# Who multiplies the last tile's branches by their mixture weights: VectorE in two wide calls, or ScalarE in sixteen narrow ones

## What is computed

```python
# _gate: four weights per token and head
w = jax.nn.softmax(logits / t, -1)
w = jnp.maximum(w, floor)
w = w / w.sum(-1, keepdims=True)
# behind it, in _L0_attn_ref: the sum of the branches by their weights,
# a root-mean-square norm over the 64 channels of each head, then the projection Wo
```

## Time and profile before

| what | value |
|---|---|
| median of 3 runs | 1334.34 us (1330.45 to 1338.84) |
| profiled execution, its own time | 1321.46 us |
| its span, first to last instruction | 1319.8 us |
| PE busy | 1152.2 us, 87% of the span |
| DVE busy | 806.1 us, 61% |
| ACT busy | 547.3 us, 41% |
| POOL busy | 395.3 us, 30% |

### The profile page before, as it was taken

The page is one execution under the profiler, slowest core; times in us unless marked ns, Lnnn a source line. Parts: engine busy times, 40 slices in busy tenths (PEclk is TensorE's granted clock), DMA queues, the critical chain, the costliest instruction groups (busy, mean ns, idle before and its releaser), DMA issues.

```text
span 1319.8 us, 25278 instructions
## 1 busy us (share of the span) xinstructions
PE 1152.2 (87%) x10204; PEld 826.6 (63%) x10204; DVE 806.1 (61%) x1542; ACT 547.3 (41%) x965; POOL 395.3 (30%) x637
## 2 busy tenths in 40 slices
PE   3778599899988998889997999889997999887828
PEld 3644485488636884378745885478735885477427
DVE  6753266765766565765776666765775666653253
ACT  1154236443563335443463336533463336531312
POOL 6007300941058100751038200841048100840000
PEclk9988799989998998989998999989997999985758
DMA  5040104010131103010040204010130104010000
GB/s 142 17 91 8 31 17 97 1 31 17 52 62 22 26 17 86 11 31 17 17 96 1 47 17 90 7 31 18 33 81 17 32 1 92 5 31 17 1 0 17
DMA packets 80244, 47.17 MB, mean 36 GB/s; under 512 B 55808, under 2 KB 73728, under 8 KB 80128
## 3 DMA queue, kind: packets, MB, share of 16 engines
q1 hardware_dynamic: 80128, 45.56, 15.2%
HBM read 30.86 MB, written 14.68 MB: 35 GB/s over the span
## 4 chain that ended last, share of the span: by engine, by line
PE 61%; DVE 20%; ACT 8%; issue 4%; POOL 3%; SPq 2%; DMA 1%; DVEq 0%; POOLq 0%; ACTq 0%
PE psum L765 12%; PE psum L766 10%; PE psum L767 10%; DVE conv_acc L1338 6%; PE psum L796 4%; DVE arena L1571 3%; PE psum L1072 3%; PE psum L951 3%; PE psum L936 2%; PE psum L970 2%; PE psum L975 2%; ACT arena L567 2%; SPq L342 2%; DVE arena L1295 2%; DVE arena L1573 1%
## 5 line engine op out<-in xcount | busy, mean ns | idle before, releaser
L512 POOL TENSOR_TENSOR l_prod<-arena 64x30 f32<-64x30 f32 (+14 forms) x240 | 145.0, 604 | 629.4 <-DMA arena<-l_dram 611.2
L563 ACT ACTIVATE h_f<-psum,b_col 128x512 f32<-128x512 f32 x128 | 87.9, 687 | 238.0 <-PE psum L767 231.3
L765 PE MATMUL psum<-w_hi,h_hi 128*128 128x256 f32 x512 | 152.5, 298 | 8.8 <-DVE h_lo L1318 8.7
L516 POOL TENSOR_TENSOR arena<-arena,l_prod 64x30 f32<-64x30 f32 (+14 forms) x240 | 150.8, 628 | 18.8
L767 PE MATMUL psum<-w_hi,h_lo 128*128 128x256 f32 x512 | 144.8, 283 | 0.0
L766 PE MATMUL psum<-w_lo,h_hi 128*128 128x256 f32 x512 | 144.7, 283 | 0.0
L1072 PE MATMUL psum<-v_shift,fir_w 128*32 128x512 f32 x1152 | 142.7, 623 | 0.0
L765 PE MATMUL psum<-xt_hi,w_hi 128*128 128x512 f32 x256 | 116.3, 454 | 22.0 <-DVE xt_lo L1304 13.2
L796 PE MATMUL psum<-ident,arena 128*128 128x128 f32 x384 | 58.7, 309 | 79.9 <-DVE arena L1295 39.7
L1338 DVE SCALAR_TENSOR_TENSOR conv_acc<-psum,conv_col,conv_acc 128x511 f32<-128x511 f32 x144 | 107.8, 749 | 32.3 <-ACT conv_acc L588 21.6
L1317 DVE CAST h_hi<-h_f 128x512 fp32r<-128x512 f32 x128 | 62.0, 484 | 100.0 <-ACT h_f L563 55.2
(11 more groups left out here) (229 smaller groups left out, 2247.9 us busy)
## 6 DMA issues: line engine op xcount, KB each, us to landing
x_in<-in_L_attn_x SPq DMA_DIRECT2D x8, 512.0 KB, 4.0
v_dram<-v_fm SPq DMA_DIRECT2D x8, 512.0 KB, 2.8
v_shift<-v_dram SPq DMA_DIRECT2D x8, 512.0 KB, 5.0
out<-x_tok SPq DMA_DIRECT2D x8, 512.0 KB, 2.9
v_shift<-v_dram SPq DMA_DIRECT2D x8, 511.0 KB, 6.9
v_shift<-v_dram SPq DMA_DIRECT2D x8, 510.0 KB, 9.1
v_shift<-v_dram SPq DMA_DIRECT2D x8, 509.0 KB, 10.9
arena<-in_L_ffn_w SPq DMA_DIRECT2D x2, 1024.0 KB, 7.4
```

Of the source, the lines that this page charges most:

```text
L512: pool.tensor_tensor(prod, l_inv[:, k + 1:, k:k + 1].broadcast_to(shape), l_inv[:, k:k + 1, 0:k].broadcast_to(shape), ALU.mult).then_inc(i ...
L516: pool.tensor_tensor(l_inv[:, k + 1:, 0:k], l_inv[:, k + 1:, 0:k], prod, ALU.add).then_inc(inverted, 1)
L563: act.activation(h_f[:, m % 2, :], bank, ACT.Gelu, bias=b1_col[:, m:m + 1]).then_inc(read, 1)
L765: pe.matmul(dst, a_hi, b_hi, start=first, stop=False, **kw)
```

## The change

ScalarE gets, directly behind the exponential, a wait for a new semaphore `mix_w_made` and sixteen calls that multiply the last tile's four units by four branches, 64 elements each, in place. VectorE releases `mix_w_made` when the weights are ready, multiplies only the first twelve units (the other three tiles), and waits for `mix_scaled`, which ScalarE's last call releases, before it adds the two tensors. Everything else stays.

```diff
@@ ScalarE
                     act.wait_ge(lshift_made, i + 1)
                     act.activation(lg[:, :, :], lg[:, :, :], ACT.Exp).then_inc(exp_made, 1)
+
+                    act.wait_ge(mix_w_made, i + 1)
+                    for u in range(HEADS * (TILES - 1), UNITS):
+                        for b in range(BR):
+                            src = (f_tok, dv_tok)[b // 2]
+                            last = act.activation(src[:, u, b % 2, :], src[:, u, b % 2, :], ACT.Identity, scale=mix_w[:, u, b:b + 1])
+                    last.then_inc(mix_scaled, 1)
                 if at.front:
                     silu(4)
                     silu(5)
@@ VectorE
                     link(dve.tensor_tensor(mix_w[:, :, :], lg[:, :, :], per_row(linv[:, :], BR), ALU.mult))
-
+                    dve.sem_inc(mix_w_made, 1)
+
+                    mine = HEADS * (TILES - 1)
                     for src, s in ((f_tok, 0), (dv_tok, 2)):
-                        link(dve.tensor_tensor(src[:, :, :, :], src[:, :, :, :],
-                                               mix_w[:, :, s:s + 2].unsqueeze(3).broadcast_to([P, UNITS, 2, D]), ALU.mult))
+                        link(dve.tensor_tensor(src[:, 0:mine, :, :], src[:, 0:mine, :, :],
+                                               mix_w[:, 0:mine, s:s + 2].unsqueeze(3).broadcast_to([P, mine, 2, D]), ALU.mult))
+                    dve.wait_ge(mix_scaled, i + 1)
                     link(dve.tensor_tensor(f_tok[:, :, :, :], f_tok[:, :, :, :], dv_tok[:, :, :, :], ALU.add))
```

More of the change, by code:

```diff
@@ L305, in macaron_kernel @@
         exp_made = sem("exp_made")
+        mix_w_made = sem("mix_w_made")
+        mix_scaled = sem("mix_scaled")
         mix_made = sem("mix_made")
```

## The result

The changed kernel takes 1343.65 us (median of 20 runs) against 1327.88 us for the kernel before (median of 20). The ratio used from here on is 1.0075, with a 95% interval from 1.0042 to 1.0109, so some 10 us slower. It leaves out every execution more than 1.5% above the fastest of its kernel, eight of the changed kernel's twenty (the profiled one of 1351.25 us among them) and one of the other's, so the medians of all twenty lie further apart, 15.8 us. The forecast was 9.1 us slower, 1343.4 us.

A forecast was written before the change was run, and what follows sets the result against it. Bound: the chain over VectorE's weights, multiplications and additions, ScalarE's Square and VectorE's scaling to TensorE's mix_t. +32.2 - 23.9 + 1.4 - 0.6 = +9.1 us on 1334.3 gave 1343.4 us; 8 in 10 range 1335 to 1354.

The forecast's parts named there:

- New stall at the norms of q: TensorE waits for ScalarE's squares of q, queued behind the sixteen calls: 4.6 us in seven passes, 32.2 us more.
- Old stalls gone: TensorE's waits at mix_t in the seven passes with front work vanish: 23.9 us less.
- VectorE's gain worth nothing where front work stands beside it: The addition starts 0.9 us earlier, worth nothing in seven passes, since ScalarE's Square waits for the rows.
- the tail pass: Last pass, no front work beside it and nothing queued behind the sixteen calls: a gain of 0.6 us.
- The clock: TensorE's lower clock behind the new stall loses 1.9 us per pass against 1.7 before: 1.4 us more in all.
- rival (b): TensorE's clock hardly falls behind the new stall: 1330 us; chance 0.14 with what lies between it and the forecast.
- (a): TensorE's clock stays low longer behind the new stall, losing 2.8 to 3.3 us: 1350 to 1354 us; chance 0.19.
- GpSimd is not in this chain.: After mix_t all stays as before, only shifted, with GpSimd not involved; no cost was counted for it.
- rival e: On ScalarE a drain comes with the SiLU's table load behind the calls: 1.38 us more per pass, 1353 us; chance 0.04.
- Rival (d): ScalarE's sixteen calls don't overlap: 5.5 us instead of 3.9, 1.6 more in each of seven passes, 1355 us; chance 0.05.

The follow-up runs named there:

- e3_three_tiles: Kernel before, with VectorE multiplying three tiles and nobody the last, whose branches are added without their weights: ratio 0.9938, 8.2 us faster.
- repeated run: The changed kernel unaltered, run a second time beside the kernel before: median 1345.3 us, ratio 1.0103.
- e2_wait_only: Kernel before plus only ScalarE's wait for the weights behind the exponential; VectorE multiplies everything, ScalarE makes no calls: ratio 0.9994.
- e9_cover: Changed kernel with five of nine slots of the filters' second half written ahead of the norms of q in TensorE's program: ratio 1.0075.
- e6_before_pool_later: Kernel before with GpSimd's last inversion steps held back until VectorE has split the second hidden tile of the second feed-forward block: ratio 1.0036.
- e5_split_stall: Kernel before with TensorE waiting, ahead of the filters' second half, until VectorE has made the mixture's first addition: ratio 0.9893.

## Why the prediction was right, step by step

The mechanism held: which queue waits, for how long, and what goes away for it. That 1343.4 meets 1343.65 so closely is luck. The forecast stood on 1334.34 us for the kernel before, the median of three runs, 6.5 us above the 1327.88 of twenty; the difference forecast, 9.1, is near the 10.0 of the ratio and well under the 15.8 of the medians; and two wrong terms, named below, pull in opposite directions.

- **New stall at the norms of q.** Forecast 4.6 us per pass, 32.2 in all; measured 4.47 to 4.87, 32.3 in all. The chain that gave it held piece by piece: calls 3.93 us (3.9), squares ready 7.29 us after the weights (7.1).
- **Old stalls gone.** All seven. TensorE comes to mix_t 0.8 us after VectorE's scaling is done in the third mixture, 1.4 in the sixth and seventh (0.7).
- **VectorE's gain worth nothing where front work stands beside it.** The addition is 0.9 us earlier, as forecast, and VectorE waits 4.55 us behind it. That the gain is real when nothing is queued behind the calls, e3_three_tiles and the tail pass (0.5 us, forecast 0.6) show.
- **The clock.** Mis-sized: forecast a loss of 1.9 against 1.7, 1.4 us more in all. From the norms' start to mix_t's it is 9.26 us on average where 7.75 is full speed, so 1.5 us are lost; behind mix_t 1.7 are saved. In all 1.4 us less, not more. In the repeated run the same stretch is 9.45 us, a loss of 1.7. The level did fall in every pass, so rival (b) is out; and (a) too, for the loss is 1.5 and 1.7, not 2.8 to 3.3.
- **"GpSimd is not in this chain."** Wrong: the term was put at nothing. VectorE's split of the hidden tiles falls into GpSimd's copy, and TensorE waits for it, 10.4 us in three passes of the profiled execution and 15.8 us in seven passes of the repeated one, against none before. That the shift of 1.2 us alone brings this about is not shown: e2_wait_only, whose way to the projection is that of the kernel before, has such waits too, 4.2 us in three passes. Still, the three profiles with ScalarE's calls ahead of the SiLUs and GpSimd not held back have the most of it over the seven passes, 11.0, 15.8 and 11.4 us (e9_cover); of the other new kernels without GpSimd's added wait none has over 5.7. In the ratio less of it is seen: 7.8 of the 10 us are explained by the terms above (9.1 of 13.7 in the repetition), and 7.8 and 10.4 together are more than 10. Both profiled executions lie above the median of their kernel, so how large this cost is in the others is open.
- **The drain beside the table load** (rival e). The load begins 0.02 us after the last call and the SiLU 0.01 us behind the load, in all seven passes; no 1.38 us are seen. The 2.66 us per switch of the Trainium skill, "ScalarE: Activation LUTs", section "What ACT_TABLE_LOAD costs", don't hold here; the load's own 1.28 us do. Rival (d) is out by the 3.93 us.

## What to carry to other kernels

Before work is moved to an engine that is idle on average, read what is written behind the place where it goes, and who waits for the first thing in that queue: the same sixteen calls cost 10 us ahead of two SiLUs and gave 6.6 behind them. A stall has a price beyond its length if the clock falls behind it; here one of 3.4 us cost 1.6 more than two of half the length, and a wait that splits it, with no work moved, was worth at least as much as any change of the work itself. Where the slow stretch falls matters too: ahead of a wait that is longer than the loss it cost nothing. And a stage that comes 1 us later meets other neighbours: look at what shared resources run beside the shifted part.

## What the runs showed of the hardware

A stall of TensorE of 3.15 to 3.9 us brought the granted clock to 0.50 behind it in all seven passes of the kernel before, but one of 3.10 us (e2_wait_only, third pass) and one of 3.25 (e6_before_pool_later, second pass) left it at 1.00. Stops of 1.3 to 2.1 us, twice per pass with 4.5 us of filters between, left it at 1.00 in five passes of e5_split_stall; in two it fell behind the first stop, of 1.83 and 1.96 us. At 2.3 to 2.8 us (e3_three_tiles) it fell in six of seven. So the length of a stall alone does not decide it.

VectorE's cast of 0.43 us took up to 5.4 us beside GpSimd's copy, memset and additions, and its subtraction of 0.69 us 5.66, waiting through several of GpSimd's instructions.

A table load of ScalarE that stands ahead of the waiting instruction costs nothing (1.28 us within a wait of 2.3 us in e2_wait_only); standing behind sixteen calls that waited themselves, it lay on the path with its 1.28 us.
